# Rounding every second half tile of a sigmoid on GpSimd instead of VectorE, in a fused attention and feed-forward kernel

## The reference

```
def fixed_qdq_u16(x):
    scale = 1.0 / 65536.0
    return jnp.clip(jnp.round(x / scale), 0.0, 65535.0) * scale
...
x = act_qdq(x)
up = act_qdq(x @ lpbq_dequant(w_up).T)
gate = act_qdq(x @ lpbq_dequant(w_gate).T)
sig = fixed_qdq_u16(jax.nn.sigmoid(gate))
gate = act_qdq(gate * sig)
o = act_qdq(gate * up)
return o @ lpbq_dequant(w_down).T
```

## Time and profile before

| | |
|---|---|
| median of 3 runs | 1347.23 us (1347.1 to 1347.79) |
| the profiled execution | 1349.18 us, its span 1347.4 us |
| PE busy | 1211.7 us, 90% of the span |
| DVE busy | 1206.0 us, 90% |
| ACT busy | 829.9 us, 62% |
| POOL busy | 559.7 us, 42%, nearly all of it before 782 us |
| sigmoid stage | 927.6 to 1072.4 us from the span's start |

### The profile page before, as it was taken

The page is one execution under the profiler, slowest core; times in us unless marked ns, Lnnn a source line. Parts: engine busy times, 40 slices in busy tenths (PEclk is TensorE's granted clock), DMA queues, the critical chain, the costliest instruction groups (busy, mean ns, idle before and its releaser), DMA issues. The chain is left out here.

```text
span 1347.4 us, 27802 instructions
## 1 busy us (share of the span) xinstructions
PE 1211.7 (90%) x8963; PEld 801.1 (59%) x8995; DVE 1206.0 (90%) x3603; ACT 829.9 (62%) x1336; POOL 559.7 (42%) x1357
## 2 busy tenths in 40 slices
PE   5689999999999999999997659998999799959998
PEld 3457777777777777777775434443433344428887
DVE  3799999999999999999997559997999989988886
ACT  2256666666676666666674346664777599974332
POOL 1177777787887878787786410000000000000000
PEclk9599999999999999999998779998999999988999
DMA  2546464555546464655544102222555455556765
GB/s 79 157 119 184 134 184 140 173 153 155 168 142 189 133 192 137 171 159 150 172 129 140 43 32 93 99 112 105 187 187 187 163 190 196 187 177 205 242 218 171
DMA packets 132369, 207.27 MB, mean 154 GB/s; under 512 B 11159, under 2 KB 97050, under 8 KB 126106
## 3 DMA queue, kind: packets, MB, share of 16 engines
q1 hardware_dynamic: 132250, 205.86, 48.6%
HBM read 125.60 MB, written 79.69 MB: 152 GB/s over the span
## 5 line engine op out<-in xcount | busy, mean ns | idle before, releaser
L671 DVE CUSTOM_DVE_ANT_0 psum<-psum,band 128x178 f32<-128x178 f32 x1024 | 317.0, 372 | 25.0 <-PE psum L880 23.6
L552 ACT ACTIVATE probs<-psum 128x356 f32<-128x356 f32 x512 | 212.4, 474 | 175.8 <-PE psum L897 175.8
L1090 PE MATMUL psum<-xnT,w_upT 128*128 (+1 forms) x1152 | 260.9, 384 | 19.1 <-DVE maxima L1314 8.8
L485 POOL TENSOR_SCALAR_AFFINE_SELECT probs<-probs 128x154 f32<-128x154 f32 (+1 forms) x512 | 224.9, 453 | 75.7 <-ACT probs L552 72.7
L1090 PEld LDWEIGHTS psum<-xnT,w_upT 128*128 128x128 f16 x1152 | 109.6, 99 | 170.2 <-issue 32.4
L494 POOL TENSOR_SCALAR_AFFINE_SELECT probs<-probs 128x254 f32<-128x254 f32 (+1 forms) x512 | 188.8, 392 | 0.0
L880 PE MATMUL psum<-k_stack,q_stack 96*128 96x178 bf16 x1024 | 137.3, 246 | 23.2 <-DVE smax L671 21.2
L897 PE MATMUL psum<-q_stack,k_stack 98*128 98x178 bf16 x1024 | 129.6, 243 | 15.3 <-DMA q_stack<-shiftT 7.2
L1690 PE MATMUL psum<-w_downT,xnT 128*128 128x256 f16 x1152 | 128.2, 275 | 16.0 <-DVE xnT L1640 16.0
L671 DVE DVE_READ_ACCUMULATOR2_ANT smax<- 128x1 f32 x1024 | 142.0, 139 | 0.0
L923 PE MATMUL psum<-probs,V 128*32 128x178 f32 x2048 | 131.1, 324 | 6.2 <-POOL probs L494 3.2
(11 more groups left out here) (189 smaller groups left out, 2262.5 us busy)
## 6 DMA issues: line engine op xcount, KB each, us to landing
k_parts_scratch<-k_parts SPq DMA_DIRECT2D x32, 384.0 KB, 2.5
q_parts_scratch<-q_parts SPq DMA_DIRECT2D x32, 384.0 KB, 2.6
k_stack<-k_parts_scratch SPq DMA_DIRECT2D x32, 384.0 KB, 4.2
q_stack<-q_parts_scratch SPq DMA_DIRECT2D x32, 384.0 KB, 5.1
gate_scratch<-g_stage SPq DMA_DIRECT2D x16, 768.0 KB, 3.3
g_in<-gate_scratch SPq DMA_DIRECT2D x16, 768.0 KB, 4.6
sig_scratch<-w_gateT SPq DMA_DIRECT2D x32, 384.0 KB, 2.3
sig_again<-sig_scratch SPq DMA_DIRECT2D x32, 384.0 KB, 3.4
```

The lines of the kernel that those rows point to most:

```text
L485: nc.gpsimd.affine_select(out=t[:, :, 0:n], in_=t[:, :, 0:n], pattern=[[0, 2], [1, n]], compare_op=ALU.is_ge, fill=0.0, base=WINDOW - off, ...
L552: nc.scalar.activation(ring_tile(probs, b, pair, c)[:].rearrange("p e j -> p (e j)"), scoreT_bank[c][:, 0:2 * SPAN], ACT.Exp, scale=DK ** ...
L671: ins = nc.vector.tensor_tensor_reduce(out=mine, in0=mine, in1=keep["band"][:, t, :], scale=1.0, scalar=-3e38, op0=ALU.add, op1=ALU.max, a ...
L1090: last = nc.tensor.matmul(bank[:], weights[wp][:, c * I + f * P:c * I + (f + 1) * P], x_parts[:, c, bass.ds(j * (2 * TILE) + xp * TILE, TI ...
```

## The change

For h = 1, POOL does the rounding that DVE did. DVE keeps the rounding of h = 0. Because the two halves now finish on different engines, `sig_rounded` becomes one semaphore for each half.

```diff
+            BY_POOL = (1,)
...
-            sig_rounded, silu_done = sem2("sig_rounded"), sem2("silu_done")
+            sig_rounded, silu_done = [sem2(f"sig_rounded{k}") for k in range(2)], sem2("silu_done")
...
-                        sp.wait_ge(sig_rounded, 2 * j + h + 1)
+                        sp.wait_ge(sig_rounded[h], j + 1)
...
+                def round_sig(j, h):
+                    pool.wait_ge(sig_done, 2 * j + h + 1)
+                    if j:
+                        pool.wait_ge(sig_stored[h], 16 * j)
+                        pool.wait_ge(silu_done, 2 * j + h - 1)
+                    nc.gpsimd.tensor_scalar(sig_int[h], sig[h][:], 65536.0, 65535.0, ALU.mult, ALU.min)\
+                        .then_inc(sig_rounded[h], 1)
+
+                for j in range(TILES):
+                    for h in BY_POOL:
+                        round_sig(j, h)
...
                 def size_of_silu(j, h):
                     u = 2 * j + h
-                    dve.wait_ge(sig_rounded, u + 1)
+                    dve.wait_ge(sig_rounded[h], j + 1)
...
-                        round_sig(j, h)
+                        if h not in BY_POOL:
+                            round_sig(j, h)
```

More of the change, by code:

```diff
@@ L1308, in round_sig @@
                     nc.vector.tensor_scalar(sig_int[h], sig[h][:], 65536.0, 65535.0, ALU.mult, ALU.min)\
-                        .then_inc(sig_rounded, 1)
+                        .then_inc(sig_rounded[h], 1)
                 def size_of_up(j, h):
```

## The result

The changed kernel takes 1392.03 us (median of 3 runs, 1391.08 to 1393.13), against 1347.23 before. The ratio is 1.0315, with a 95% interval of 1.0292 to 1.0337. I had forecast slower, at 1357.2 us and at most 1376. The direction held and the size did not: +44.8 us instead of +10.

A forecast was written before the change was run, and what follows sets the result against it. DVE was taken to bound the sigmoid stage. Its +6.1 us (tiles 1 to 14 +5.3, tile 0 -0.4, tile 15 +1.2) and +3.9 for the second config instruction gave +10.0 on 1347.23: 1357.2 us, range 1344.5 to 1376.

The forecast's parts named there:

- DVE sets the pace: Sigmoid stage: DVE, busy for all of 20 us, bounds the kernel there, at 8.54 us for each tile.
- PE binds at 7.77 us: Sigmoid stage: a relieved DVE would need 7.67 us, so PE's 7.77 limits the gain to 0.77 us for each tile.
- W: POOL's time for one rounding of 1536 elements in the sigmoid stage: 2.1 us, with bounds 0.95 and 3.4.
- Whoever is first holds the other for nearly the whole instruction: Sigmoid stage: POOL and DVE's two-SBUF-input size_of_silu exclude each other; half 0's starts 1.25 us late.
- my formula: Sigmoid stage: a tile's length is 6.82 + W, or 8.92 us against 8.54, so 0.38 us longer.
- 15 x 5.37 - 21.5: The forecast's total change in us as a function of W, 15 W - 21.5, with W at 5.37; forecast +10.0.
- Tile 0, "-0.4": Sigmoid stage's first tile: 0.4 us shorter, with POOL's rounding in DVE's gap and the first config instruction hidden.
- The last tile, W - 0.91: Sigmoid stage's tile 15: POOL, held by size_of_silu, ends later than DVE's last rounding did; +1.2 us.
- The second config instruction, +3.9, bounds to 5.1: Start of the next stage: POOL's reduction comes 5.05 us later, of which 1.17 come back; +3.9 us, bounds 3.9 to 5.1.
- The slow POOL: Rival, sigmoid stage: W over 2.6, +17.5 to +29.5 us, 1365 to 1377; chance 0.24.
- That the custom instruction isn't held: Rival, sigmoid stage: POOL doesn't hold size_of_silu, the tile is 7.77 us, -7.1 us, 1340.1; chance 0.06.
- a second config instruction that is free: Rival, next stage's start: the second config instruction costs nothing or is hidden, +6.1 us, 1353.3; chance 0.07.

The follow-up runs named there:

- the version with ACT: Against the kernel before: ACT instead of DVE rounds half 1, as a Copy with factor 65535.99 behind its own sigmoid; 1334.67 us, ratio 0.9903.
- POOL's cast: The changed kernel, where POOL only casts half 1's 1536 columns to 16 bits, without factor and clip; 1342.63 us, beside 1350.05 for the kernel before.
- the widths tried: The changed kernel with POOL rounding 768, 1024 or 1152 of half 1's 1536 columns, DVE the others; 1358.41, 1357.0 and 1389.04 us.
- 1024 columns: The changed kernel with POOL rounding 1024 columns of half 1 and DVE the other 512; 1357.0 us, beside 1356.47 for the kernel before.
- the run with POOL's prices: The kernel before with 21 POOL instructions, three each of seven forms, added in the gate stage where POOL is idle; 1361.34 us.
- the unused reduction: The kernel before plus a one-column POOL tensor_scalar in the sigmoid stage and, right behind it, a partition reduction whose result nothing uses; ratio 1.0003.
- 1152: The changed kernel with POOL rounding 1152 columns of half 1 and DVE the other 384; 1389.04 us, beside 1356.47 for the kernel before.
- 768 columns on POOL: The changed kernel with POOL rounding 768 columns of half 1 and DVE the other 768; 1358.41 us, beside 1350.05 for the kernel before.

## Why the prediction was right in direction and wrong in size

- **"DVE sets the pace", and PE binds at 7.77 us.** Right: relieved without a hold, DVE let the tile fall to 7.77 us (the version with ACT).
- **"I take W = 2.1, because the select also reads one SBUF tensor, and keep 0.95 and 3.4".** This is the step that failed. W measured 5.37. The number of inputs was not what the nearest row had to share. POOL's price goes by the kind of instruction: tensor_scalar costs 3.4 ns for each element where the select costs 1.22. The upper bound was a row of yet another kind, and so no bound. I had no row for W and should have let the upper end be open. Why this kind is so slow stays open. The Trainium skill ("GPSIMD Engine Reference", section "Performance versus the Vector engine") has such a body near the pace of its reads, an estimated 1.3 us; measured are 5.39 and 5.37 us for two operations, and 4.09 for one. The page's figure does not hold for this instruction; the cast, at 1.47 us, comes near it.
- **"Whoever is first holds the other for nearly the whole instruction".** Right in kind for `size_of_silu`, the custom instruction: it is held, and the order of starts decides who is held. That only two SBUF inputs matter isn't so: DVE's reductions and L650 went free with one, its casts and roundings did not. In length it was right for POOL's cast (0.2 us before the end), wrong for the rounding (1.5 before the end): POOL lets `size_of_silu` go on while it is still at work, by the widths tried when it has read its last block. With W = 5.37 my formula would give 12.2 us for the tile, and it was 10.84. So the error of the hold took back part of that of W: 15 x 5.37 - 21.5 would have been +59 us. The Trainium skill ("SBUF — State Buffer", section "Who interferes with whom") calls the shared pair an exclusive lock and says, of DVE's two-port modes, that the other one blocks for the whole instruction. The runs agree in who blocks whom. For `size_of_silu` they show a shorter hold beside the slow tensor_scalar: until 0.85 us after POOL's start with 1024 columns, of 3.88.
- **Tile 0, "-0.4".** It was +1.0. The step that failed is that the first config instruction "would be over at 934.5": POOL stood 9.3 us and not 5.57. How much of it is the reload is open. In the run with POOL's prices, the first tensor_scalar had no sigmoid to wait for and began 7.35 us after the end of the memset ahead of it. In the sigmoid stage POOL always began 2.0 to 2.6 us after the sigmoid was ready, and that came 7.2 us behind the config instruction in every run.
- **The last tile, W - 0.91.** Right: 4.46 by the measured W, 4.3 measured.
- **The second config instruction, +3.9, bounds to 5.1.** Right in mechanism, at 5.4 to 5.5 us in size, a little outside. The time to the reduction was 6.8 to 6.9 us there and not 5.57; the 1.1 us that came back were as foretold. I did not try what made it longer; DMA loads ran beside it, but with loads of another kind beside it the unused reduction began 5.7 us behind its config instruction. "Against it is the one such row" was not the whole of the trace of before: a config instruction at L485, at 71.0, was followed by POOL's next instruction at 71.12. So not every config instruction costs something, and the rival deserved that mention.
- **The rivals.** The slow POOL was the case that came true, but beyond its own upper end. That the custom instruction isn't held fell, and so did a second config instruction that is free.

## What to carry to other kernels

A POOL instruction must be priced by its own kind: a cast of 1536 columns took 1.47 us and a two-operation tensor_scalar of the same tile 5.37, and no neighbour of another kind bounds either. Work moved from DVE to POOL comes back as waiting where POOL works while DVE has two SBUF inputs, or rounds or casts from one, and busy time doesn't show that; look at the longest duration of a line beside its median. Where an engine has room and doesn't hold DVE, as ACT had here with 14.4 of 20 us, the work belongs there.

## What the runs showed of the hardware, unexpected

- POOL's tensor_scalar seems to read in blocks of 1024 columns of f32, one ahead of the calculation. DVE was held 0.14 us with 1024 columns and 2.85 with 1152. The block is inferred from four widths; nothing shows it directly. A one-operation form also let go 1.0 us before its end; other types of input weren't tried.
- A one-input rounding of DVE was held by POOL too, for 3.9 us in one place (4.24 instead of 0.35 us), though a tensor_reduce and a scalar_tensor_tensor with one SBUF input went free.
- The config instruction costs differently from place to place. POOL stood 9.1 to 9.8 us ahead of the first tensor_scalar of the sigmoid stage and 7.35 in the gate stage. From the config instruction to a reduction it was 5.5 to 7.6 us. At the start of the next stage it was 6.8 to 7.0, and 7.4 with 768 columns on POOL. At L485 it cost nothing to speak of. A cast after a reduction needed none.
- A second operation in POOL's tensor_scalar costs 1.28 us on 1536 columns (4.09 to 5.37). The type of the output costs nothing.
